# Per-half maxima in an attention softmax: two factors behind the cast and a summed total, in place of a running maximum

## The chip, the cores and the metric

The kernel runs on one core of one Trainium2 chip. The metric is the device time of one execution in microseconds; the time before is the median of three runs. The profile shows one further execution, which also has its own time.

## The reference, cut to what matters

For each of 4 batch rows (2048 positions, width 256, 16 heads of 16), talking-heads attention mixes the heads before and after the softmax. Layer norms and a soft mixture of experts follow; they are untouched by the change.

```python
logits = jnp.einsum('bhid,bhjd->bhij', q, k) * SCALE
logits = jnp.einsum('bhij,gh->bgij', logits, Wpre)
attn = jax.nn.softmax(logits, axis=-1)
attn = jnp.einsum('bhij,gh->bgij', attn, Wpost)
out = jnp.einsum('bhij,bhjd->bhid', attn, v)
```

The softmax runs over 2048 keys. It does not change if a different maximum is subtracted in different parts of the row, as long as each part is rescaled before the sum.

## The kernel before, in words

The work is cut into tiles of 8 query positions x 16 heads = 128 partitions against all 2048 keys. A tile is handled by a `slot`; 16 slots make an iteration, 16 iterations a batch row, and 4 batch rows the kernel: 1024 tiles. The slots are software pipelined: in slot T the engines work on the scores of tile T, on the weights of tile T-1 and on the post-mix of tile T-2. Each engine has its own instruction stream with the order written out by hand in its `slot` function, and semaphores join them. Two halves of the keys are separate: the scores of tile T fill the four banks of `psS`, banks 0 and 1 for the first half, 2 and 3 for the second.

- **TensorE** (L1249 to L1283): scores of columns 0 and 1 (L1179, 12 matmuls, the head mix before the softmax folded into `AH` and `AL`), `turn` of the first half of tile T-2 (L1199, which mixes the heads and puts keys on the partitions, with `rh` and `rl` as weights, into `psP`), scores of columns 2 and 3, and `turn` of the second half. `turn` writes the two banks of `psP` again, so it waits for VectorE's `mixed_low`. Every eighth slot (t = 2 and 10) the product with V (L1214) stands in four pieces between these. The output projection `y` (L1225) is in slot 3 and other row work in slots 11, 12 and 15.
- **ScalarE** (L683): two casts `mixed_high` of `psP` (L653), `bound` (L622, the negative, scaled maximum `nb`), `exps` (L635, the exponentials of a half of the keys and their sum), `highs` (L663, the fp16 cast `ph`); then the same five for the second half, with `factor` (L644, `f0`) between its `exps` and its `highs`.
- **VectorE** (L1021): `half_max` of the first half (L816), the reciprocal of the total of tile T-1 (L848), two `mixed_low` (L830), `low` of tile T-1 (L856, 512 columns), `half_max` of the second half, `row_bound` (L822), two `mixed_low`, and `low` of tile T (L856, 1024 columns). Row work for layer norms stands between (`rows`), and `out_copy` (L840) in slots 3 and 11.
- **GpSimd** (L548): `total` (L517), `mixq` (two L438), `roots`, `first_half` (L524), `post` (L531), `mixq_high` (L446), `post_high` (L540), `mixq_low` (L451), `post_low` (L545), and `low` (L508, the last 512 columns). `roots` are the small steps of two Newton iterations for the layer norms; there are six of them in each of slots 6, 7, 10 and 11, spread over four places (two, one, two, one).

How the softmax is put together before: the first half of the keys is exponentiated against its own maximum, the second against the maximum of both (`row_bound`, a running maximum). One factor `f0 = exp(nb1 - nb0)` carries the first half over, the total is `sums0 * f0 + sums1` in one instruction, and the weights of the halves are `f0 / total` and `1 / total`. The waits that matter:

```python
a.wait_ge(s_mx, T * 3 + 2 * h + 1 + 1)   # bound: second half waits for row_bound
g.wait_ge(s_exp, T * 2 + 2 + 1)          # total
g.wait_ge(s_f, T + 1 + 1)
g.tensor_scalar(tot[:, p:p + 1], sums[:, p, 0:1], f0[:, p:p + 1], sums[:, p, 1:2],
                ALU.mult, ALU.add).then_inc(s_tot, 1)
v.wait_ge(s_tot, T + 1 + 1)              # recip, in VectorE's next slot
```

Of the kernel before, what the change touches and what calls it, by code (L numbers as in the profile page):

```python
# [29 lines left out]
ALU = mybir.AluOpType  # L30
ACT = mybir.ActivationFunctionType
X = mybir.AxisListType.X

P = 128
# [24 lines left out]
LIFT = 14  # L59
# [20 lines left out]
def seq_layer(nc, x, xT, wqk, wv, bqk, bv, wpre, wpost, imask, wout, bout, gamma, beta, mu, scale,  # L80
              w1, b1, w2, b2, cos_t, sin_t, ident_d, out):
    ctx = ExitStack()
    with ctx:
        def sb(name, shape, dt=F32):
            return ctx.enter_context(nc.sbuf_tensor(name, shape, dt))

        def sem(name):
            return ctx.enter_context(nc.semaphore(name))
# [35 lines left out]
        mu_s = sb("mu_s", [P, KT, ES])  # L124
        ident = sb("ident", [P, P])
        ones = sb("ones", [P, P])
        top = sb("top", [P, 2, 3])
        nb = sb("nb", [P, 2, 2])
        sums = sb("sums", [P, 2, 2])
        f0 = sb("f0", [P, 2])  # L130
        tot = sb("tot", [P, 2])
        rr = sb("rr", [P, 2, 2])
        rp = sb("rp", [P, 2, HP])
# [32 lines left out]
        def part(n):  # L166
# [58 lines left out]
        s_A = sem("s_A")  # L225
        s_S = sem("s_S")
        s_mx = sem("s_mx")
        s_exp = sem("s_exp")
        s_nb = sem("s_nb")
        s_f = sem("s_f")  # L230
        s_tot = sem("s_tot")
        s_rec = sem("s_rec")
# [38 lines left out]

        FROM_ONE = [s_A, s_nb, s_f, s_tot, s_rec, s_r0, s_rp, s_rh, s_rl, s_pl, s_plg, s_D, s_F, s_y, s_mx, s_exp, s_ph,
                    s_mh, s_ml, s_oc, s_CTc, s_t1, s_xb, s_st, s_nw, s_out]

        block = ctx.enter_context(nc.Block())
# [9 lines left out]
        def apart(e):  # L287

            e.sem_inc(s_carry, 1)
# [110 lines left out]
        def _(g):  # L400
# [5 lines left out]
            with g.Fori(0, B) as b:  # L406
# [21 lines left out]
                def mixq(it, t, fresh):  # L428

                    T = (b * NIT + it) * TI + t  # L430
                    if not fresh:
                        g.wait_ge(s_S, T * NC - (TG - 1) * NC)
                    g.wait_ge(s_A, T * 4 + 1)
                    for h in range(2):
                        i0 = it * (TI * QI) + (t * QI + h * HQ)
                        v = at[:, :, h * HP:(h + 1) * HP].rearrange("p k (g i) -> p k g i", g=H)
                        apart(g)
                        g.tensor_tensor(v, Q[:, :, bass.ds(i0, HQ)].unsqueeze(2).broadcast_to([P, KT, H, HQ]),  # L438
                                        wpre_q[:, :].unsqueeze(1).unsqueeze(3).broadcast_to([P, KT, H, HQ]),
                                        ALU.mult).then_inc(s_A, 1)  # L440
# [62 lines left out]
                def low(T, t, early):  # L503

                    g.wait_ge(s_ph, T * 2 + 2 + 1)
                    if not early:
                        g.wait_ge(s_D, (T - 1) * 2 + 1)
                    g.tensor_tensor(pl[:, t % 2, NL:N], pr[:, t % 2, NL:N], ph[:, t % 2, NL:N],  # L508
                                    ALU.subtract).then_inc(s_plg, 1)

                def total(T, t):

                    p = t % 2
                    g.wait_ge(s_exp, T * 2 + 2 + 1)
                    g.wait_ge(s_f, T + 1 + 1)
                    apart(g)
                    g.tensor_scalar(tot[:, p:p + 1], sums[:, p, 0:1], f0[:, p:p + 1], sums[:, p, 1:2],  # L517
                                    ALU.mult, ALU.add).then_inc(s_tot, 1)

                def first_half(T, t):  # L520

                    p = t % 2
                    g.wait_ge(s_rec, T + 1 + 1)
                    g.tensor_tensor(rr[:, p, 0:1], rr[:, p, 1:2], f0[:, p:p + 1], ALU.mult).then_inc(s_r0, 1)  # L524

                def post(T, t):

# [20 lines left out]
                def slot(it, t, first, work, live=True):  # L548

                    T = (b * NIT + it) * TI + t  # L550
                    one = not (first and t < 1)
                    t_1 = (t - 1) % TI
                    if one:
                        total(T - 1, t_1)
                    if live:
                        mixq(it, t + LEAD, first and t + LEAD < TG)
                    roots(t, work, 0)
                    if one:
                        first_half(T - 1, t_1)
                        post(T - 1, t_1)  # L560
                    if live:
                        mixq_high(it, t + LEAD)
                    if one:
                        post_high(T - 1, t_1, first and t < 5)
                    if live:
                        mixq_low(it, t + LEAD)
                    if one:
                        post_low(T - 1, t_1)
                    roots(t, work, 1)
                    if one:  # L570
                        low(T - 1, t_1, first and t < 3)
                    roots(t, work, 2)
                    if work is not None and t == POOL_SLOT["bias"]:
                        add_bias(work)
                    roots(t, work, 3)
# [20 lines left out]
        def _(a):  # L596
            barrier(a, 1)
            with a.Fori(0, B) as b:
# [18 lines left out]
                def bound(T, t, h):  # L617

                    p = t % 2
                    m = 2 * h  # L620
                    a.wait_ge(s_mx, T * 3 + 2 * h + 1 + 1)
                    a.activation(nb[:, p, h:h + 1], top[:, p, m:m + 1], ACT.Copy, bias=LIFT * math.log(2.0),  # L622
                                 scale=-SSCALE).then_inc(s_nb, 1)

                def exps(T, t, h, early):
# [13 lines left out]
                def factor(T, t, early):  # L639

                    p = t % 2
                    if not early:
                        a.wait_ge(s_r0, T - 2 + 1 + 1)
                    a.activation(f0[:, p:p + 1], nb[:, p, 0:1], ACT.Exp, bias=nb[:, p, 1:2], scale=-1.0).then_inc(s_f, 1)  # L644

                def mixed_high(T, t, c, Gd):

# [35 lines left out]
                def slot(it, t, first, work, live=True):  # L683


                    T = (b * NIT + it) * TI + t
                    G = (b * NIT + it) * 2
                    early = first and t < 2

                    def mixed(c):  # L690
                        if not (first and t < 2):
                            mixed_high(T - 2, (t - 2) % TI, c, G + (t - 2) // TG)

                    mixed(0)
                    mixed(1)
                    if live:
                        bound(T, t, 0)
                        exps(T, t, 0, early)
                        highs(T, t, 0, early)
                    mixed(2)  # L700
                    mixed(3)
                    if live:
                        bound(T, t, 1)
                        exps(T, t, 1, early)
                        factor(T, t, early)
                        highs(T, t, 1, early)
                    if work is not None and t == ACT_SLOT["turn_u"]:
                        turn(work)
                    if work is not None and t == ACT_SLOT["weigh"]:
                        weigh(work)  # L710
                    if work is not None and t == ACT_SLOT["turn_c"]:
                        store_c(work)
# [26 lines left out]
        def _(v):  # L739
# [39 lines left out]
            with v.Fori(0, B) as b:  # L779
# [36 lines left out]
                    v.tensor_reduce(top[:, t % 2, h:h + 1], psS[:, 2 * h:2 * h + 2, :].rearrange("p c n -> p (c n)"),  # L816
                                    X, ALU.max).then_inc(s_mx, 1)

                def row_bound(T, t):

                    v.wait_ge(s_mx, T * 3 + 2 + 1)
                    v.tensor_tensor(top[:, t % 2, 2:3], top[:, t % 2, 0:1], top[:, t % 2, 1:2], ALU.max).then_inc(s_mx, 1)  # L822

                def mixed_low(T, t, c):

                    v.wait_ge(s_mh, T * NC + c + 1 + 1)
# [17 lines left out]
                def recip(T, t):  # L844

                    p = t % 2
                    v.wait_ge(s_tot, T + 1 + 1)
                    v.reciprocal(rr[:, p, 1:2], tot[:, p:p + 1]).then_inc(s_rec, 1)  # L848

                def low(T, t, h, early):  # L850

# [169 lines left out]
                def slot(it, t, first, work, live=True):  # L1021


                    T = (b * NIT + it) * TI + t
                    two = not (first and t < 2)
                    one = not (first and t < 1) and (live or t < 1)
                    t_1, t_2 = (t - 1) % TI, (t - 2) % TI
                    if live:
                        half_max(T, t, 0)
                    if one:  # L1030
                        recip(T - 1, t_1)
                    rows(t, work, 0)
                    if t % TG == 3 and not (first and t < TG):
                        out_copy((b * NIT + it) * 2 + t // TG - 1, (t // TG + 1) % 2, b * NIT + it - (1 if t < TG else 0))
                    if two:
                        mixed_low(T - 2, t_2, 0)
                        mixed_low(T - 2, t_2, 1)
                    rows(t, work, 1)
                    if one:
                        low(T - 1, t_1, 1, first and t < 3)  # L1040
                    if live:
                        half_max(T, t, 1)
                        row_bound(T, t)
                    rows(t, work, 2)
                    if two:
                        mixed_low(T - 2, t_2, 2)
                        mixed_low(T - 2, t_2, 3)
                    if live:
                        low(T, t, 0, first and t < 2)
                    rows(t, work, 3)  # L1050
# [348 lines left out]
```

## Time and profile before

| what | value |
|---|---|
| median of 3 runs | 8940.56 us (8935.8 to 8940.84) |
| profiled execution, its own time | 8924.24 us |
| its span, first to last instruction | 8922.4 us |
| busy: TensorE, VectorE, ScalarE, GpSimd | 8352.7, 8136.2, 7237.5, 5892.5 us |
| TensorE's mean granted clock | 0.985 of full |

Busy time is what an engine's instructions took, waits at a semaphore left out. An instruction that has started but is held by something on the chip still counts as busy. The time that the kernel takes is decided by which engine others wait for, and that differs between stretches.

### The profile page before, as it was taken

What the parts mean: (1) busy time and instruction counts of PE and PEld (TensorE: products, weight loads), DVE (VectorE), ACT (ScalarE), POOL (GpSimd) and SP (SyncE); (2) the same over time, 40 slices, a digit from 0 to 9 for tenths busy, and PEclk for the clock granted to TensorE, in tenths of its full rate; (3) what the DMA queues carried; (4) which work ended last, traced back from release to release, by engine and by line L of the source; (5) the groups of instructions that cost most, each with busy time, mean ns of one, the idle gap of its engine ahead of it and who ended that gap; (6) DMA issues with size and microseconds to landing.
All of it is one profiled execution on the core that took longest, in us unless ns stands there. A gap on an engine that the chain in (4) does not pass through costs nothing.

```text
span 8922.4 us, 398983 instructions
## 1 busy us (share of the span) xinstructions
PE 8352.7 (94%) x158060; PEld 4650.8 (52%) x158060; DVE 8136.2 (91%) x12237; ACT 7237.5 (81%) x13696; POOL 5892.5 (66%) x12005
## 2 busy tenths in 40 slices
PE   8999999998899999999889999999989999999997
PEld 4555555555455555555545555555554555555554
DVE  7999999997899999999789999999978999999997
ACT  6888888886688888888668888888856888888885
POOL 6666666764666676666466667666646666766673
PEclk9999999999999999999899999999989999999998
DMA  0000000002000000000200000000020000000002
GB/s 31 7 8 8 8 8 8 9 7 73 17 8 8 8 9 7 8 9 8 72 17 8 8 8 9 7 8 9 8 72 17 8 8 8 9 8 8 8 9 76
DMA packets 98673, 141.22 MB, mean 16 GB/s; under 512 B 7840, under 2 KB 88352, under 8 KB 94496
## 3 DMA queue, kind: packets, MB, share of 16 engines
q1 hardware_dynamic: 96800, 115.48, 3.8%
q8 instruction: 1270, 20.81, 1.0%
q14 instruction: 603, 4.94, 0.2%
HBM read 73.51 MB, written 39.85 MB: 13 GB/s over the span
## 4 chain that ended last, share of the span: by engine, by line
DVE 44%; PE 33%; issue 19%; DVEq 2%; ACT 1%; POOL 1%; POOLq 0%; ACTq 0%
PE psS L1179 17%; DVE top L816 14%; DVE big L830 14%; DVE pl L856 9%; PE psP L1199 6%; PE psO L1214 6%; PE psM L1225 1%; DVE top L822 1%; ACT big L653 1%; DVE rr L848 1%; PE psS L1311 1%; PE psS L1340 1%; DVEq L815 0%; DVEq L853 0%; PE psS L1151 0%
## 5 line engine op out<-in xcount | busy, mean ns | idle before, releaser
L830 DVE SCALAR_TENSOR_TENSOR big<-psP,big 128x512 f16<-128x512 f32 x4096 | 2605.9, 675 | 285.0 <-ACT big L653 275.8
L816 DVE TENSOR_REDUCE top<-psS 128x1 f32<-128x1024 f32 x2048 | 2479.7, 1211 | 214.0 <-PE psS L1179 213.7
L653 ACT ACTIVATE big<-psP 128x512 f16<-128x512 f32 x4096 | 2199.2, 589 | 577.5 <-PE psP L1199 572.4
L1179 PE MATMUL psS<-KH,AH 128*128 128x512 f16 x8192 | 2464.3, 383 | 43.5 <-POOL AL L451 41.8
L1179 PE MATMUL psS<-KH,AL 128*128 128x512 f16 x8192 | 2441.9, 380 | 0.0
L1179 PE MATMUL psS<-KL,AH 128*128 128x512 f16 x8192 | 2439.2, 379 | 0.0
L635 ACT ACTIVATE pr<-psS,nb 128x1024 f32<-128x1024 f32 x2048 | 2281.3, 1114 | 69.1 <-ACT nb L622 3.0
L663 ACT ACTIVATE ph<-pr 128x1024 f16<-128x1024 f32 x2048 | 2151.9, 1051 | 32.3
L1199 PEld LDWEIGHTS psP<-rh,ph 64*128 64x128 f16 x32768 | 1434.3, 95 | 1220.1 <-DVE big L830 1036.0
L1199 PE MATMUL psP<-rh,ph 64*128 64x64 f16 x32768 | 1682.5, 192 | 381.8 <-DVE big L830 344.5
L517 POOL TENSOR_SCALAR tot<-sums,f 128x1 f32<-128x1 f32 x1024 | 743.7, 726 | 1946.6 <-ACT f L644 1943.3
L856 DVE TENSOR_TENSOR pl<-pr,ph 128x1024 f16<-128x1024 f32 (+1 forms) x2048 | 2020.2, 986 | 0.0
L1199 PE MATMUL psP<-rh,pl 64*128 64x64 f16 x32768 | 1663.0, 190 | 0.7 <-issue 0.6
L1199 PE MATMUL psP<-rl,ph 64*128 64x64 f16 x32768 | 1662.9, 190 | 0.3 <-issue 0.2
L1199 PEld LDWEIGHTS psP<-rl,ph 64*128 64x128 f16 x32768 | 1463.2, 95 | 1.8 <-issue 1.6
L1199 PEld LDWEIGHTS psP<-rh,pl 64*128 64x128 f16 x32768 | 1462.7, 95 | 1.2 <-issue 1.1
L1179 PEld LDWEIGHTS psS<-KH,AL 128*128 128x128 f16 x8192 | 802.9, 98 | 971.5 <-issue 6.6
L1179 PEld LDWEIGHTS psS<-KL,AH 128*128 128x128 f16 x8192 | 802.8, 98 | 970.1 <-issue 6.6
L508 POOL TENSOR_TENSOR pl<-pr,ph 128x512 f16<-128x512 f32 x1024 | 1210.2, 1182 | 0.0
L1179 PEld LDWEIGHTS psS<-KH,AH 128*128 128x128 f16 x8192 | 629.2, 98 | 608.4 <-POOL AL L451 43.4
L622 ACT ACTIVATE nb<-top 128x1 f32<-128x1 f32 x2048 | 418.2, 204 | 559.1 <-DVE top L822 434.7
L451 POOL TENSOR_TENSOR AL<-at,AH 128x256 f16<-128x256 f32 x1024 | 798.1, 779 | 2.8
(135 smaller groups left out, 7956.0 us busy)
## 6 DMA issues: line engine op xcount, KB each, us to landing
ph<-in_xT SPq DMA_DIRECT2D x16, 512.0 KB, 7.9
xr<-in_x SPq DMA_DIRECT2D x64, 128.0 KB, 2.1
Q<-in_w SPq DMA_DIRECT2D x8, 1024.0 KB, 6.4
out<-V SPq DMA_DIRECT2D x16, 512.0 KB, 3.9
d_x<-x SPq DMA_DIRECT2D x60, 128.0 KB, 1.7
d_xn<-xn SPq DMA_DIRECT2D x60, 128.0 KB, 1.7
d_lg<-lg SPq DMA_DIRECT2D x60, 128.0 KB, 1.7
d_ct<-cT SPq DMA_DIRECT2D x60, 128.0 KB, 1.7
```

What stands on the lines that cost most here:

```text
L451: g.tensor_tensor(AL[:, t % TG, :, :], at[:, :, :], AH[:, t % TG, :, :], ALU.subtract).then_inc(s_A, 1)
L508: g.tensor_tensor(pl[:, t % 2, NL:N], pr[:, t % 2, NL:N], ph[:, t % 2, NL:N], ALU.subtract).then_inc(s_plg, 1)
L517: g.tensor_scalar(tot[:, p:p + 1], sums[:, p, 0:1], f0[:, p:p + 1], sums[:, p, 1:2], ALU.mult, ALU.add).then_inc(s_tot, 1)
L635: a.activation(pr[:, p, h * N2:(h + 1) * N2], psS[:, 2 * h:2 * h + 2, :].rearrange("p c n -> p (c n)"), ACT.Exp, bias=nb[:, p, h:h + 1], s ...
L653: a.activation(PT[:, hf * JH:(hf + 1) * JH, :, 0, i0:i0 + HQ], psP[:, ih, :].rearrange("p (j g i) -> p j g i", j=JH, g=H), ACT.Copy, scale ...
L663: a.activation(ph[:, t % 2, cs], pr[:, t % 2, cs], ACT.Copy).then_inc(s_ph, 1)
L816: v.tensor_reduce(top[:, t % 2, h:h + 1], psS[:, 2 * h:2 * h + 2, :].rearrange("p c n -> p (c n)"), X, ALU.max).then_inc(s_mx, 1)
L830: v.scalar_tensor_tensor(out=PT[:, js, :, 1, i0:i0 + HQ], in0=psP[:, ih, :].rearrange("p (j g i) -> p j g i", j=JH, g=H), scalar=MDROP, in ...
L856: v.tensor_tensor(pl[:, t % 2, cs], pr[:, t % 2, cs], ph[:, t % 2, cs], ALU.subtract)\
L1179: mm = pe.matmul(psS[:, c, :], A_[:, k8, k, :], K_[:, k, c * CW:(c + 1) * CW], start=n == 0, stop=n == 5)
L1199: mm = pe.matmul(psP[:, ih, j * HP:(j + 1) * HP], p_[rows, t % 2, cs], r_[rows, t % 4, hf, :], start=n == 0, stop=n == 2, tile_position=(i ...
L1214: mm = pe.matmul(psO[32 * w:32 * w + 32, q * P:(q + 1) * P], V[:, j, g_, :, :], PT[:, j, g_, :, :], start=j == 0 and q == 0, stop=j == JT - 1,
```

## The change

Each half keeps its own maximum. `row_bound` on VectorE goes, and ScalarE's `bound` of the second half waits for `half_max` alone. GpSimd gets `lower_bound` (the smaller of the two `nb`) at the head of its slot, then `mixq`, and only then `total`, which is now two instructions: both sums times their factors, and their addition. `factor` makes both factors in one instruction, waits for `lower_bound`, and stands behind `highs` of the second half. `weights` makes both weights in one instruction from the reciprocal.

```diff
 # GpSimd
+                def lower_bound(T, t):
+                    p = t % 2
+                    g.wait_ge(s_nb, T * 2 + 2 + 1)
+                    apart(g)
+                    g.tensor_scalar(nm[:, p:p + 1], nb[:, p, 0:1], nb[:, p, 1:2], None, ALU.min).then_inc(s_nm, 1)
+
                 def total(T, t):
                     p = t % 2
                     g.wait_ge(s_exp, T * 2 + 2 + 1)
                     g.wait_ge(s_f, T + 1 + 1)
-                    apart(g)
-                    g.tensor_scalar(tot[:, p:p + 1], sums[:, p, 0:1], f0[:, p:p + 1], sums[:, p, 1:2],
-                                    ALU.mult, ALU.add).then_inc(s_tot, 1)
-
-                def first_half(T, t):
+                    g.tensor_tensor(ws[:, p, :], sums[:, p, :], ff[:, p, :], ALU.mult).then_inc(s_ws, 1)
+                    g.wait_ge(s_ws, T + 1 + 1)
+                    g.tensor_tensor(tot[:, p:p + 1], ws[:, p, 0:1], ws[:, p, 1:2], ALU.add).then_inc(s_tot, 1)
+
+                def weights(T, t):
                     p = t % 2
                     g.wait_ge(s_rec, T + 1 + 1)
-                    g.tensor_tensor(rr[:, p, 0:1], rr[:, p, 1:2], f0[:, p:p + 1], ALU.mult).then_inc(s_r0, 1)
+                    g.tensor_tensor(rr[:, p, :], ff[:, p, :], rc[:, p:p + 1].broadcast_to([P, 2]), ALU.mult)\
+                     .then_inc(s_r0, 1)
...
                     if one:
-                        total(T - 1, t_1)
+                        lower_bound(T - 1, t_1)
                     if live:
                         mixq(it, t + LEAD, first and t + LEAD < TG)
+                    if one:
+                        total(T - 1, t_1)
                     roots(t, work, 0)
                     if one:
-                        first_half(T - 1, t_1)
+                        weights(T - 1, t_1)
                         post(T - 1, t_1)
 # ScalarE
                 def bound(T, t, h):
                     p = t % 2
-                    m = 2 * h
-                    a.wait_ge(s_mx, T * 3 + 2 * h + 1 + 1)
-                    a.activation(nb[:, p, h:h + 1], top[:, p, m:m + 1], ACT.Copy, bias=LIFT * math.log(2.0),
+                    a.wait_ge(s_mx, T * 2 + h + 1 + 1)
+                    a.activation(nb[:, p, h:h + 1], top[:, p, h:h + 1], ACT.Copy, bias=LIFT * math.log(2.0),
                                  scale=-SSCALE).then_inc(s_nb, 1)
...
                 def factor(T, t, early):
                     p = t % 2
+                    a.wait_ge(s_nm, T + 1 + 1)
                     if not early:
                         a.wait_ge(s_r0, T - 2 + 1 + 1)
-                    a.activation(f0[:, p:p + 1], nb[:, p, 0:1], ACT.Exp, bias=nb[:, p, 1:2], scale=-1.0).then_inc(s_f, 1)
+                    a.activation(ff[:, p, :], nb[:, p, :], ACT.Exp, bias=nm[:, p:p + 1], scale=-1.0).then_inc(s_f, 1)
...
                         exps(T, t, 1, early)
+                        highs(T, t, 1, early)
                         factor(T, t, early)
-                        highs(T, t, 1, early)
 # VectorE
-                def row_bound(T, t):
-
-                    v.wait_ge(s_mx, T * 3 + 2 + 1)
-                    v.tensor_tensor(top[:, t % 2, 2:3], top[:, t % 2, 0:1], top[:, t % 2, 1:2], ALU.max).then_inc(s_mx, 1)
...
                     v.wait_ge(s_tot, T + 1 + 1)
-                    v.reciprocal(rr[:, p, 1:2], tot[:, p:p + 1]).then_inc(s_rec, 1)
+                    v.reciprocal(rc[:, p:p + 1], tot[:, p:p + 1]).then_inc(s_rec, 1)
...
                         half_max(T, t, 1)
-                        row_bound(T, t)
```

## Rows read from the trace of the kernel before

**Rows 1.** The page's first part, busy time of each engine.

```profile
PE 8352.7 (94%) x158060; PEld 4650.8 (52%) x158060; DVE 8136.2 (91%) x12237; ACT 7237.5 (81%) x13696; POOL 5892.5 (66%) x12005
```

**Rows 2.** Waits, whole span: who for whom, total us, times, longest us.

```profile
POOL tot L517 <- ACT f L644: 1943.3, 952, 5.2
...
PE psP L1199 <- DVE big L830: 344.5, 520, 2.6
...
POOL rr L524 <- DVE rr L848: 359.7, 724, 1.5
...
POOL rp L531 <- POOL rr L524: 212.7, 1024, 0.5
```

**Rows 3.** Windows: stretch, us, busy us by engine (instructions), clock, DMA.

```profile
4022.20:4152.10 129.90, 124.67 (x2450) 68.79 (x2449) 122.44 (x183) 111.73 (x212) 89.47 (x187) 1.00 0.03 8
4030.30:4068.20 37.90, 35.34 (x602) 18.36 (x597) 37.73 (x63) 34.16 (x65) 28.56 (x61) 1.00 0.03 10
4129.40:4157.40 28.00, 27.98 (x673) 16.83 (x673) 24.08 (x33) 22.11 (x43) 17.06 (x34) 1.00 0.01 4
```

**Rows 4.** The chain that ended last, behind an output product: start, us, what.

```profile
4143.24 1.01 PE psO L1214 x64
4144.24 0.81 PE psP L1199 x48
4145.05 2.70 PE psS L1179 x12
```

**Rows 5.** Groups of instructions by shape: busy us, mean ns, idle time before them.

```profile
L822 DVE TENSOR_TENSOR top<-top 128x1 f32<-128x1 f32 x1024 | 748.0, 730 | 35.5
...
L644 ACT ACTIVATE f<-nb 128x1 f32<-128x1 f32 x1024 | 289.7, 283 | 0.0
```

**Rows 6.** VectorE's timeline in a slot that it paces: start, us, what.

```profile
4045.93 1.21 DVE L816 TENSOR_REDUCE top<-psS 128x1 f32<-128x1024 f32 x1
4047.17 1.04 DVE L822 TENSOR_TENSOR top<-top 128x1 f32<-128x1 f32 x1
4048.14 1.27 DVE L830 SCALAR_TENSOR_TENSOR big<-psP,big 128x512 f16<-128x512 f32 x2
4049.34 1.21 DVE L856 TENSOR_TENSOR pl<-pr,ph 128x1024 f16<-128x1024 f32 x1
```

**Rows 7.** GpSimd's timeline over the same slot and the next one.

```profile
4047.05 1.15 POOL L508 TENSOR_TENSOR pl<-pr,ph 128x512 f16<-128x512 f32 x1
...
4050.07 0.69 POOL L517 TENSOR_SCALAR tot<-sums,f 128x1 f32<-128x1 f32 x1 [1.18 <-ACT f L644]
4050.72 0.76 POOL L438 TENSOR_TENSOR at<-Q,wpre_q 128x128 f32<-128x128 f32 x2
...
4057.60 0.34 POOL L517 TENSOR_SCALAR tot<-sums,f 128x1 f32<-128x1 f32 x1
```

**Rows 8.** ScalarE's timeline from the end of a second turn on.

```profile
4161.00 1.08 ACT L653 ACTIVATE big<-psP 128x512 f16<-128x512 f32 x2
4162.06 0.20 ACT L622 ACTIVATE nb<-top 128x1 f32<-128x1 f32 x1
...
4163.40 0.28 ACT L644 ACTIVATE f<-nb 128x1 f32<-128x1 f32 x1
4163.59 1.05 ACT L663 ACTIVATE ph<-pr 128x1024 f16<-128x1024 f32 x1
4164.54 1.08 ACT L653 ACTIVATE big<-psP 128x512 f16<-128x512 f32 x2
```

**Rows 9.** Single lines: count, duration in ns, min/median/max.

```profile
L822 DVE TENSOR_TENSOR top<-top x1024: 158/879/1146, 86.1 to 8820.4; 128x1 f32<-128x1 f32 x171
...
L517 POOL TENSOR_SCALAR tot<-sums,f x1024: 334/683/1338, 93.7 to 8822.9; 128x1 f32<-128x1 f32 x171
...
L469 POOL TENSOR_TENSOR zq<-yq x192: 185/190/643, 291.0 to 8854.2; 128x1 f32<-128x1 f32 x192
```

**Rows 10.** VectorE's timeline at the start of a batch.

```profile
94.06 0.16 DVE L848 RECIPROCAL rr<-tot 128x1 f32<-128x1 f32 x1 [5.02 <-POOL tot L517]
```

More of the change, by code:

```diff
@@ L126, in seq_layer @@
         ones = sb("ones", [P, P])
-        top = sb("top", [P, 2, 3])
+        top = sb("top", [P, 2, 2])
         nb = sb("nb", [P, 2, 2])
         sums = sb("sums", [P, 2, 2])
-        f0 = sb("f0", [P, 2])
+        nm = sb("nm", [P, 2])
+        ff = sb("ff", [P, 2, 2])
+        ws = sb("ws", [P, 2, 2])
+        rc = sb("rc", [P, 2])
         tot = sb("tot", [P, 2])
@@ L229, in seq_layer @@
         s_nb = sem("s_nb")
+        s_nm = sem("s_nm")
+        s_ws = sem("s_ws")
         s_f = sem("s_f")
@@ L270, in seq_layer @@
         s_out = sem("s_out")
-        FROM_ONE = [s_A, s_nb, s_f, s_tot, s_rec, s_r0, s_rp, s_rh, s_rl, s_pl, s_plg, s_D, s_F, s_y, s_mx, s_exp, s_ph,
+        FROM_ONE = [s_A, s_nb, s_nm, s_ws, s_f, s_tot, s_rec, s_r0, s_rp, s_rh, s_rl, s_pl, s_plg, s_D, s_F, s_y, s_mx, s_exp, s_ph,
                     s_mh, s_ml, s_oc, s_CTc, s_t1, s_xb, s_st, s_nw, s_out]
```

## The prediction

> **What bounds the kernel now.** I start with the share of the engines in the page [rows 1]: TensorE is busy 94% of the span and VectorE 91%, so neither is free to absorb much, and the question is who waits for whom. The waits of TensorE come next [rows 2]: by far the largest is the post-mix transposition (L1199) waiting for VectorE's `mixed_low` (L830), 344.5 us in 520 cases. That is what a faster VectorE can give back, and no more: a TensorE that never waited there would still need its 8352.7 us busy and its other idle time.
>
> The windows show the two regimes [rows 3]. One whole iteration of 16 slots lasts 129.9 us with TensorE busy for 124.7, so 5.2 us are lost (344.5 / 64 iterations = 5.4). In the nearly five slots behind the `y` product, 37.9 us, VectorE is busy 37.7 and TensorE 35.3: VectorE sets the pace. In the 28 us around the first output product TensorE is busy 28.0 and VectorE 24.1. A plain slot on TensorE is two groups of twelve score matmuls at 2.70 us and two turns at 0.81 [rows 4], 7.02 us; the iteration averages 8.1.
>
> Why VectorE is slow is in its timeline [rows 6]. L816 for the second half starts at 4045.93, L822 (the running maximum, one element a partition) at 4047.17, and the next L830 only at 4048.14. L822 alone, 1.04 us, ends at 4048.21; GpSimd's L508 started at 4047.05 and took 1.15 us, so it ended at 4048.20 [rows 7]. The same instruction takes 0.158 us at its shortest [rows 9] and 0.730 in the mean of 1024 [rows 5]; its median is 0.879 [rows 9], so in most slots it waits, and in this one for L508. The Trainium skill's page "SBUF — State Buffer", section "Who interferes with whom", states this: a VectorE instruction with two SBUF inputs and a GpSimd instruction that reads SBUF exclude each other, and the one that starts second waits for the whole of the first. By that rule, the trace agrees here.
>
> **The change, part by part.**
>
> *L822 goes.* On VectorE an instruction moves the next start by its duration less 0.07 (the pair of L830, 1.27 long, by 1.20, rows 6). From L816's start at 4045.93 to L830's at 4048.14 are 2.21 us; less 1.14 for L816 that leaves 1.07 for an L822 of 1.04. So one costs its duration and 0.03: 0.76 us in the mean, 16 x 0.76 = 12.2 us an iteration, on VectorE, and ScalarE's second bound (L622), which waits for it, comes as much earlier. VectorE's need falls from about 122 to 110 us an iteration [rows 3], below TensorE's 124.7. VectorE alone would then cost TensorE nothing: all 344.5 us would come back. The stall could move to the next instruction of its kind, L856, which starts 2.2 us after L822's place (4049.34 against 4047.17, rows 6), while L508 is over after 1.15; taken as 0, at most the 0.57 us that L822 loses now (0.730 - 0.158).
>
> *Lower bound (new) on GpSimd.* One `tensor_scalar` on one element. Its bounds are L517's: 0.34 where nothing holds it, 1.34 where L856 does [rows 9]. GpSimd waits 1.9 us a slot for ScalarE's L644 today (1943.3 us over 1024 slots, rows 2; 1.18 at 4050.07, a slot after root work), so 0.3 is hidden; I take 0.3, by the minimum, since the lower bound falls where VectorE runs L830 and not L856. ScalarE's `factor` now waits for it, and behind it stand the two L653 of the next slot.
>
> *`mixq` moves ahead of the total.* 0.76 us [rows 7] go from behind the total into GpSimd's wait: free there, and the reciprocal is not reached later by it as long as GpSimd gets to it before the factors are there. L446, AL and all behind keep their order.
>
> *The factors move behind the cast L663.* Two elements in place of one, 0.28 us either way [rows 5] (bounds 0.20, the bound's L622, and 0.29). They come one cast later: L663 starts at 4163.59 and the next instruction 0.95 later [rows 8]. The cast itself comes 0.19 earlier. ScalarE's total is unchanged.
>
> *The total is two instructions.* Each `tensor_tensor` of one or two elements lies between 0.19 and 0.64 [rows 9], with a 0.20 us gap where one waits for the other on GpSimd (L531 behind L524, 212.7 us in 1024, rows 2): 0.19 + 0.20 + 0.19 = 0.58 against 0.34 unhindered for L517 (median 0.68, since L856 often holds it). The two-wide weights cost the same 0.19 as L524: 0.
>
> *The ring that the new order makes.* The end of a second turn on TensorE starts ScalarE's casts (L653, 4161.00), bound (4162.06), exponentials, then cast and factors: 4163.40 + 0.95 + 0.28 = 4164.63 [rows 8]. GpSimd starts some 0.2 later (the same gap as above): total done at 4164.85 + 0.58 = 4165.43. Reciprocal (0.16, rows 10) and two `mixed_low` (1.20, rows 6) bring 4166.8. The turn before ended just ahead of 4161.00, and TensorE wants its next second turn 7.02 - 0.81 = 6.2 us later, at 4167.2. So in a plain slot the ring fits, with 0.3 to 0.5 us to spare. Before, factor and total were 1.2 us earlier in it.
>
> *Where it doesn't fit: the Newton steps.* In slots 6, 7, 10 and 11 GpSimd has six small instructions more, about 1.5 us with gaps. There it is full: from L517 at 4050.07 to L517 at 4057.60, 7.53 us without a wait for the factor [rows 7]. New: 7.53 - 0.34 + 0.30 + 0.58 = 8.07, 1.05 over TensorE's slot. The first of a run starts with GpSimd's idle time in hand (1.9 less the new 0.3 and a little, 1.5), so it ends up some 0.5 late, which the ring's spare swallows; the second (slot 7) is 1.0 late for real. Slot 10 lies under the output product, which adds four times 1.01 us on TensorE [rows 4], and slot 11 is again a first one. That leaves 1.0 us an iteration. I add 0.5 for small VectorE work between reciprocal and L830 (`variances` in slot 5, the output copy in 3 and 11), which the short spare no longer hides: 1.5 x 60 = 90 us.
>
> *Starts and ends of the four batches.* At a start VectorE waits 5.02 us for the total [rows 10], which now has the lower bound and `mixq` in front of it; at an end the last factors are a cast later. About 1.5 + 1.0 us, 4 times: 10 us.
>
> *Sum.* -344.5 + 90 + 10 = -244.5 us. The profiled execution took 8924.24: 8679.7. The median of the runs is 8940.56, 16.3 above it; I carry that over: **8696 us**, 2.7% less.
>
> **Rivals.**
>
> *A. TensorE alone sets the time.* The late totals of slot 7 vanish because slot 8 and the lead of TensorE's scores absorb them. For it: TensorE already runs without a gap around an output product (27.98 of 28.00) [rows 3] although VectorE needs 8 us a slot elsewhere, so there is more elasticity than my spare. 8940.6 - 344.5 + 10 = 8606. This is the low end.
>
> *B. GpSimd becomes the bound in every slot.* If L856 (1.21 us, rows 6) gets in between L508 and the lower bound or `mixq`, GpSimd waits it out each slot. The full slot of 7.53 us less 1.5 of root work is 6.0, the holds of L856 in it counted; new instructions add 0.54, the wait for the reciprocal 0.35 (359.7 us over 1024, rows 2), a lower bound held in full up to 0.6 more: 6.9 to 7.5, and 8.1 to 8.7 with root work. With 0.2 us a slot over TensorE in ten slots and 1.3 in three that is 5.9 us an iteration, less 1 to 4 of slack: a gain of 0 to 230 us, about 110: 8830. For it: L517 has a median of 0.683 against 0.34 unhindered, so GpSimd meets L856 there today. Against: with L822 gone L508 starts before L856 by a wide margin, and in TensorE's pace two L830 lie between. The page named above gives the rule by which this would happen: its lock is exclusive and held for a whole instruction, so new GpSimd instructions can lose 1.1 us each; by it alone the sum would be this 8830.
>
> *C. Slower.* One mechanism: the lower bound falls behind L856 (1.34 us instead of 0.3), ScalarE stands at `factor`, and L653, which TensorE needs, stands behind it. It decides once the factor is later than today's slot of 8.1 us allows: the ring of 6.7 us (with the turn itself) would need 1.4 us more in nearly every slot, not just the 1.0 that one L856 costs. With two of them, 0.1 us over 8.1 in 900 slots: 9030.
>
> *D. The gain is under 0.2%*: B at its worst; 8925 to 8940.
>
> **How the numbers follow.** 0.2% (18 us) is about what a measurement of this kernel can tell from no change. My own case 0.45 (8650 to 8780), A 0.20 (8600 to 8650), B 0.20 (8780 to 8920), D 0.08, C 0.07. The likeliest is my own: 8696. The range for 8 in 10 goes from A's end, 8600, to 8890, inside B. Faster 0.84, same 0.09, slower 0.07.
>
> **What would show it.** In the profile after: L822's row gone and VectorE's busy time about 750 us lower; TensorE's wait for L830 down from 344.5 to about 100 us; L856's mean unchanged within 0.1; GpSimd's largest wait still that for the factor (shorter, some 1 us a slot), and a new wait of VectorE's reciprocal for the total that is concentrated in slots 7, 8 and 12. B would show as GpSimd busy or held without waits for the factor, and the reciprocal waiting in most slots; C as a wait of L644 for the lower bound in most slots; A as TensorE's wait near nothing. I am wrong on mechanism if TensorE still waits 250 us or more.

## The result and the profile after

The median went from 8940.19 to 8837.6 us, a ratio of 0.9891 (95% interval 0.9878 to 0.9905): 1.1% faster, where 2.7% were forecast. The direction was right and the size was less than half. The profiled execution took 8836.91 us, its span 8835.1.

The page's first part, as [rows 1], and the waits of the whole span, as [rows 2]:

```profile
PE 8342.3 (94%) x158060; PEld 4654.2 (53%) x158060; DVE 7730.8 (88%) x11213; ACT 7314.1 (83%) x13696; POOL 6557.3 (74%) x14053
```

```profile
POOL nm L521 <- ACT nb L636: 494.7, 396, 4.8
POOL ws L528 <- ACT ff L659: 474.5, 619, 2.2
...
PE psP L1208 <- DVE big L840: 274.1, 432, 3.0
...
DVE rc L858 <- POOL tot L530: 164.8, 195, 6.3
...
ACT ff L659 <- POOL nm L521: 99.8, 128, 5.5
```

TensorE still waits 274.1 us for `mixed_low` (now L840) where I forecast about 100; the prediction had named 250 or more as the sign of a wrong mechanism. VectorE's busy time fell by 405 us, not by the 748 that L822 had. GpSimd is busy 665 us longer. ScalarE's `factor` (L659) waits for the lower bound 128 times, about twice an iteration, and VectorE's reciprocal for the total 195 times. As forecast, that wait is concentrated in slots 7, 8 and 12: 45.9, 66.5 and 19.5 of the 164.8 us.

The groups of instructions show where 227 of VectorE's missing 343 us went (count, busy us, mean ns), and what `mixq` takes now:

```profile
L866 DVE TENSOR_TENSOR pl<-pr,ph 128x1024 f16<-128x1024 f32 x1024 | 1306.2, 1276 | 0.0
L443 POOL TENSOR_TENSOR at<-Q,wpre_q 128x128 f32<-128x128 f32 x2048 | 1241.2, 626 | 9.2 <-POOL AL L456 5.0 <-issue 2.3 <-POOL Q L429 1.6
...
L866 DVE TENSOR_TENSOR pl<-pr,ph 128x512 f16<-128x512 f32 x1024 | 850.0, 830 | 0.0
...
L973 DVE TENSOR_TENSOR colmax<-colmax,lg 128x256 f32<-128x256 f32 x64 | 70.7, 1104 | 0.0
...
L909 DVE TENSOR_SCALAR ir<-vr 128x2 int32<-128x2 int32 x64 | 57.2, 894 | 0.1
```

In the kernel before, the same instructions were (the groups of that trace; L856 is now L866, L438 is L443, L963 is L973, L899 is L909):

```profile
L856 DVE TENSOR_TENSOR pl<-pr,ph 128x1024 f16<-128x1024 f32 x1024 | 1238.1, 1209 | 0.0
...
L856 DVE TENSOR_TENSOR pl<-pr,ph 128x512 f16<-128x512 f32 x1024 | 782.2, 764 | 0.0
L438 POOL TENSOR_TENSOR at<-Q,wpre_q 128x128 f32<-128x128 f32 x2048 | 781.9, 400 | 7.0 <-POOL AL L451 5.0 <-POOL Q L424 1.5
...
L963 DVE TENSOR_TENSOR colmax<-colmax,lg 128x256 f32<-128x256 f32 x64 | 26.3, 411 | 0.0
...
L899 DVE TENSOR_SCALAR ir<-vr 128x2 int32<-128x2 int32 x64 | 10.0, 156 | 0.1
```

The hold moved. VectorE's L909 went from 156 to 894 ns and L973 from 411 to 1104, both forms of L866 took 0.07 us more, and on GpSimd `mixq` (L443) went from 400 to 626 ns. In the trace before, no L899 and no L963 starts more than 0.1 us ahead of the end of GpSimd's L508: L822 stood in front of them and took the hold. In the trace after, 56 of the 64 L909 and 60 of the 64 L973 start inside GpSimd's L513, and end 0.02 to 0.03 and 0.28 to 0.29 us behind its end. VectorE's timeline in slot 13, and GpSimd's beside it, show the first kind:

```profile
4058.70 1.21 DVE L831 TENSOR_REDUCE top<-psS 128x1 f32<-128x1024 f32 x1
4059.84 1.25 DVE L973 TENSOR_TENSOR colmax<-colmax,lg 128x256 f32<-128x256 f32 x1
4061.01 1.27 DVE L840 SCALAR_TENSOR_TENSOR big<-psP,big 128x512 f16<-128x512 f32 x2
```

```profile
4059.65 1.15 POOL L513 TENSOR_TENSOR pl<-pr,ph 128x512 f16<-128x512 f32 x1
4060.79 0.45 POOL L521 TENSOR_SCALAR nm<-nb 128x1 f32<-128x1 f32 x1
```

L973 stands where L822 stood, right behind the maximum of the second half. It starts at 4059.84 inside GpSimd's L513 (to 4060.80), and ends 0.29 us behind that, at 4061.09.

**Where TensorE waits, slot by slot.** The idle time of TensorE ahead of its turns (L1199, after L1208), summed over the trace by the slot that the scores before it belong to. The first turn and the second are apart, the figures are mean us per iteration of the 60 with row work, and figures under 0.05 are left out. The two last columns are totals in us: the four first iterations of the batches, which have no row work, and the turns behind the last scores of a batch. The first turn of a slot waits for the `mixed_low` pair at the end of VectorE's slot before, so a late row instruction of slot 5, 8 or 13 shows in slot 6, 9 or 14. The second turn waits for the pair right behind the reciprocal, so a late total shows there.

```
slot            0    1    3    6    7    8    9    14   15   sum   | first its.  ends
before  turn 1  .29  .53  -    .43  .93  -    .75  .86  .81  4.60  |
        turn 2  -    -    -    -    -    -    .30  -    -    0.31  |  38.8      34.2
after   turn 1  -    -    -    .31  -    -    .83  .70  -    1.84  |
        turn 2  -    -    .32  -    .71  .78  .30  -    -    2.18  |   1.6      35.0
```

Before: 4.91 x 60 + 38.8 + 34.2 = 368 us. After: 4.02 x 60 + 1.6 + 35.0 = 278 us. The difference is 90 us, and the spans differ by 87, but they aren't made of the same waits. Of the 38.8 us in the first iterations 22.0 are waits for GpSimd's `rl` (4 times, at the starts of the batches). After the change TensorE waits 21.8 us for ScalarE's `pr` at its scores, where it was 1.4, so most of these 22 only moved. The wait for `mixed_low` fell by 70.4 us (16.8 to 1.6 of it in the first iterations), and TensorE's busy time by 10.4. The windows confirm the iterations without row work. The first iteration of the second batch and the one behind it, in the kernel before and in the kernel after:

```profile
2299.95:2427.56 127.61, 117.44 (x1984) 60.87 (x1985) 109.66 (x147) 102.51 (x193) 89.16 (x176) 0.97 0.01 2
2427.56:2557.86 130.30, 124.94 (x2455) 68.95 (x2450) 122.44 (x183) 111.73 (x212) 89.99 (x187) 1.00 0.02 6
```

```profile
2276.91:2399.62 122.71, 116.71 (x1985) 60.57 (x1985) 101.58 (x132) 103.23 (x193) 102.60 (x206) 0.97 0.01 3
2399.62:2528.71 129.09, 124.81 (x2454) 68.96 (x2449) 116.23 (x167) 112.89 (x212) 100.26 (x219) 1.00 0.02 6
```

In this pair of windows the iteration without row work gains 4.9 us, the one with it 1.2.

### The profile page after: what moved, and what is told of

Its sections match the earlier page's. It is cut to its first block, busy times and chain, and to the rows that moved or that the text cites. A ratio compares the mean times of both kernels' runs of the same rounds, so it can differ in the third digit from the quotient of the medians.

```text
span 8835.1 us, 399633 instructions
## 1 busy us (share of the span) xinstructions
PE 8342.3 (94%) x158060; PEld 4654.2 (53%) x158060; DVE 7730.8 (88%) x11213; ACT 7314.1 (83%) x13696; POOL 6557.3 (74%) x14053
## 4 chain that ended last, share of the span: by engine, by line
PE 51%; DVE 21%; issue 16%; POOL 7%; ACT 4%; DVEq 1%; POOLq 1%; ACTq 0%
PE psS L1188 29%; PE psP L1208 11%; DVE big L840 6%; PE psO L1223 6%; DVE pl L866 5%; DVE top L831 5%; ACT big L668 3%; PE psM L1234 1%; POOL rh L553 1%; POOL zr L476 1%; POOL zr L474 1%; PE psS L1320 1%; PE psS L1349 1%; POOL at L443 1%; POOL rl L558 1%
## 5 line engine op out<-in xcount | busy, mean ns | idle before, releaser
L840 DVE SCALAR_TENSOR_TENSOR big<-psP,big 128x512 f16<-128x512 f32 x4096 | 2614.6, 678 | 439.7 <-ACT big L668 424.8
L866 DVE TENSOR_TENSOR pl<-pr,ph 128x1024 f16<-128x1024 f32 (+1 forms) x2048 | 2156.2, 1053 | 0.0
L1208 PEld LDWEIGHTS psP<-rh,ph 64*128 64x128 f16 x32768 | 1433.0, 95 | 1102.1 <-DVE big L840 852.3
L1208 PE MATMUL psP<-rh,ph 64*128 64x64 f16 x32768 | 1681.2, 192 | 284.0 <-DVE big L840 274.1
L1208 PE MATMUL psP<-rh,pl 64*128 64x64 f16 x32768 | 1661.3, 190 | 2.6 <-issue 2.5
L1208 PE MATMUL psP<-rl,ph 64*128 64x64 f16 x32768 | 1661.2, 190 | 0.4 <-issue 0.2
L1208 PEld LDWEIGHTS psP<-rh,pl 64*128 64x128 f16 x32768 | 1461.3, 95 | 3.7 <-issue 3.5
L1208 PEld LDWEIGHTS psP<-rl,ph 64*128 64x128 f16 x32768 | 1461.9, 95 | 2.1 <-issue 2.0
L443 POOL TENSOR_TENSOR at<-Q,wpre_q 128x128 f32<-128x128 f32 x2048 | 1241.2, 626 | 9.2 <-POOL AL L456 5.0
L513 POOL TENSOR_TENSOR pl<-pr,ph 128x512 f16<-128x512 f32 x1024 | 1196.1, 1168 | 0.0
L521 POOL TENSOR_SCALAR nm<-nb 128x1 f32<-128x1 f32 x1024 | 413.1, 403 | 501.4 <-ACT nb L636 494.7
```

The costliest lines, as they stand in the source:

```text
L840: v.scalar_tensor_tensor(out=PT[:, js, :, 1, i0:i0 + HQ], in0=psP[:, ih, :].rearrange("p (j g i) -> p j g i", j=JH, g=H), scalar=MDROP, in ...
L866: v.tensor_tensor(pl[:, t % 2, cs], pr[:, t % 2, cs], ph[:, t % 2, cs], ALU.subtract)\
L1208: mm = pe.matmul(psP[:, ih, j * HP:(j + 1) * HP], p_[rows, t % 2, cs], r_[rows, t % 4, hf, :], start=n == 0, stop=n == 2, tile_position=(i ...
```

## The experiments

Three theories stood against each other at first. Theory 1: GpSimd is late in the slots with Newton steps, the lower bound with it, and ScalarE's `factor` and casts stand behind. Theory 2: L822's stall sits on VectorE's row work now. Theory 3: the ring of factor and total has become too long in plain slots too. The table above already speaks against theory 3, since slots 0, 1, 4, 5 and 10 to 13 lose nothing in the kernel after.

Times are medians; the ratios are to the kernel before, which each group of runs took again on its own chip (8930 to 8937 us). "After" stands at 0.9891 (0.9878 to 0.9905), beside a kernel before at 8940.19. A difference to it in us can therefore be off by about 10 us, and where the intervals of the ratios overlap the two versions are not told apart.

**One: the lower bound ahead of the last Newton steps.** In slot 7 of the kernel after, GpSimd's and ScalarE's timelines read:

```profile
4009.61 1.16 POOL L513 TENSOR_TENSOR pl<-pr,ph 128x512 f16<-128x512 f32 x1
4010.73 1.17 POOL L476 TENSOR_TENSOR zr<-zr,vr 128x2 f32<-128x2 f32 x1
4012.10 0.19 POOL L479 TENSOR_SCALAR zr<-zr 128x2 f32<-128x2 f32 x1 [0.20 <-POOL zr L476]
4012.38 0.19 POOL L481 TENSOR_TENSOR yr<-yr,zr 128x2 f32<-128x2 f32 x1
4012.59 0.28 POOL L521 TENSOR_SCALAR nm<-nb 128x1 f32<-128x1 f32 x1
4012.87 0.76 POOL L443 TENSOR_TENSOR at<-Q,wpre_q 128x128 f32<-128x128 f32 x2
4013.59 0.20 POOL L528 TENSOR_TENSOR ws<-sums,ff 128x2 f32<-128x2 f32 x1
```

```profile
4011.06 1.06 ACT L678 ACTIVATE ph<-pr 128x1024 f16<-128x1024 f32 x1
4012.91 0.29 ACT L659 ACTIVATE ff<-nb,nm 128x2 f32<-128x2 f32 x1 [0.79 <-POOL nm L521]
4013.11 1.06 ACT L668 ACTIVATE big<-psP 128x512 f16<-128x512 f32 x2
```

A Newton step of 0.19 us lasts 1.17 behind VectorE's L866, the lower bound is late by that, and `factor` stands 0.79 us with the casts for TensorE behind it. So the edit moves the lower bound ahead of those steps.

```diff
-                        lower_bound(T - 1, t_1)      # head of slot T
...
                         low(T - 1, t_1, first and t < 3)
+                    if not drain:
+                        lower_bound(T, t)            # end of slot T
                     roots(t, work, 2)
```

> The kernel after, with GpSimd's lower bound of tile T moved to the end of slot T, ahead of the last three Newton steps (they follow it), in place of the head of slot T+1. Theory 1 (GpSimd is late in root slots: ScalarE's factor stands for the lower bound, 99.8 us in 128 cases, and the casts L668 stand behind the factor): that wait goes to under 20 us, TensorE's wait for L840 falls from 274 to about 170, time 8837 - 100 = 8740. Theory 2 (the stall of the removed L822 sits now on VectorE's row instructions L909, L933 and L973): nothing of that is touched, 8825 to 8840. Theory 3 (the longer ring of factor and total is too long in plain slots as well): unchanged, 8830 to 8840.

Measured 8869.64, ratio 0.9927 (0.9914 to 0.9941): 32 us slower than after. The wait of `factor` went as expected, but nothing was gained:

```profile
DVE rc L858 <- POOL tot L530: 212.9, 259, 6.3
ACT nb L636 <- DVE top L831: 146.3, 254, 9.8
ACT ff L659 <- POOL nm L521: 25.4, 12, 5.6
```

The Newton steps now stand between the lower bound and the total, so VectorE's reciprocal waits longer (212.9 us against 164.8). TensorE's wait in slots 7 and 8 is 0.88 + 0.84 us, and 0.44 is new in slot 11. Theory 1 in this form falls: this order within GpSimd doesn't help. What is left of it is the amount of work ahead of the total, which run four tries.

**Two: VectorE's row work away from L822's old place.**

```diff
-                    rows(t, work, 2)
                     if two:
                         mixed_low(T - 2, t_2, 2)
                         mixed_low(T - 2, t_2, 3)
+                    rows(t, work, 2)
```

> The kernel after, with VectorE's row work of place 2 (L909, L933, L973, L983 and bn_stats) moved behind the two mixed_low of the second half, away from GpSimd's L513. Theory 2: L909 falls from 0.89 to 0.16 us in the mean and L973 from 1.10 to 0.41; of the 1.7 us an iteration that reach the path about 1 comes back at TensorE, 60 iterations: 8837 - 60 = 8775. Theory 1: the mean of L909 and L973 falls but slots 6 to 9 stay late: 8820 to 8837. Theory 3: 8830 to 8840.

Measured 8803.23, ratio 0.985 (0.9835 to 0.9865): 34 us faster than after. L973 is back at 426 ns and L909 at 396. Slots 6 and 14 lose 0.08 and 0.04 us in place of 0.31 and 0.70, while slot 15 gets 0.34; the sum is 3.44 in place of 4.02, and 0.58 x 60 = 35 us. The moved hold is real and worth this much, a little over half of the 60 us that I had expected. Slot 9 keeps 1.09 of its 1.13 us.

**Three: both moves.**

> Both moves together: the lower bound ahead of the last Newton steps, and VectorE's row work behind the second pair of mixed_low. If theories 1 and 2 are both right and separate places: the sum of the two gains, about 8680. If only one is right: the time of that one run alone. Theory 3: no more than 20 us from 8837.

Measured 8841.89, ratio 0.9897 (0.9882 to 0.9912), no different from after. The two effects add with their signs: +32 - 34.

**Four: two Newton iterations in place of three** (`NEWTON = 2`, with the steps spread as 1, 1, 1, 1 over the four places). The kernel makes three Newton iterations for each of its two roots, where its description above speaks of two in all. The roots of this version are less exact, so it is a probe and no replacement.

> The kernel after with two Newton iterations for each root in place of three (the inverse roots of the layer norms are less exact: that part of the computation is cut by a third; the rest is as in the reference). Each root slot has four small GpSimd instructions in place of six. Theory 1: 2 x 0.25 us less in each of slots 6, 7 and 11 gives back 0.5 to 1.5 us an iteration: 8837 - 60 = 8775, and the factor's wait for the lower bound falls to a third. Theory 2: L973 in slot 13 unchanged, L909 may change as GpSimd's phase does: 8800 to 8837. Theory 3: 8830.

Measured 8775.35, ratio 0.9819 (0.9806 to 0.9833): 62 us faster than after. Slots 7 and 8 lose 0.30 + 0.27 us in place of 0.71 + 0.78, and slots 6, 9 and 14 are unchanged (0.34, 0.84 + 0.30, 0.71). Two small instructions less in a slot give back 0.9 us an iteration: GpSimd's amount of work in the root slots is on the path.

**Five to eight: the order, part by part.** The change has two halves: other maxima (with lower bound, two factors and a total of two steps) and another order (`factor` behind the cast, `mixq` ahead of the total). Each half was undone alone or in part.

```diff
 # five, ScalarE
+                        factor(T, t, early)
                         highs(T, t, 1, early)
-                        factor(T, t, early)
```

```diff
 # six, GpSimd
                         lower_bound(T - 1, t_1)
+                        total(T - 1, t_1)
                     if live:
                         mixq(it, t + LEAD, first and t + LEAD < TG)
-                    if one:
-                        total(T - 1, t_1)
```

Seven has both of these edits, and eight has the new order in the kernel before, with the running maximum and `f0` kept.

> The kernel after with one part undone: ScalarE's factor stands ahead of the cast of the second half, as before the change. Theory 3 (the ring is 0.95 us too long with the factor behind the cast): the total is ready 0.95 us earlier, VectorE's reciprocal waits less (164.8 us now) and the time falls by 50 to 100: 8760. Theory 1: the factor needs the lower bound 0.95 us sooner and so stands longer for it, in plain slots too; the wait of L659 for L521 rises from 100 us to 300 or more and the time rises: 8870 to 8930.

Measured 8866.68, ratio 0.9929 (0.9916 to 0.9943), 29 us slower than after. The reciprocal waits less (104.7 us), as theory 3 had it, but the wait of `factor` for the lower bound is 336.0 us in 278 cases. The cast in front of it is useful cover.

> The kernel after with one part undone: GpSimd makes the total ahead of mixq. Theory 1: mixq (0.76 us) falls behind the wait for the factor, GpSimd's work per slot grows by what it used of that wait, root slots are 0.7 us later each and the time rises: 8870 to 8920. Theory 3: in root slots GpSimd reaches the total 0.76 us sooner, the reciprocal's wait shrinks, 8800. Theory 2: within 20 us of 8837.

Measured 8809.38, ratio 0.9867 (0.9852 to 0.9883), 28 us faster than after by the medians and 21 by the ratios, whose intervals just touch; TensorE's waits ahead of its turns are 36 us less in its trace. That is against theory 1's expectation. Theory 3 had about this time, but by a shorter wait of the reciprocal, and that wait is longer (200.5 us). Slots 7 and 8 are worse, as theory 1 says (0.97 + 1.14 us). But with GpSimd in another phase `mixq` isn't held (405 ns against 626), nor are L909 and L973 (154 and 462 ns), and slots 6, 9 and 14 lose 0.00, 0.64 and 0.06 us in place of 0.31, 1.13 and 0.70.

> Only the maximum is changed: separate maxima, lower bound, two factors and the two-step total, but the factor ahead of the cast and the total ahead of mixq, as in the kernel before. It says what the removal of L822 is worth without the new order. Theory 1: lower bound, factor and total now stand in one chain on the path of both engines; the gain over before (8940) is small or gone: 8900 to 8980. Theory 3: the short ring is kept and L822 is gone: 8750.

Measured 8914.68, ratio 0.9984 (0.9975 to 0.9993). `factor` waits 377.7 us for the lower bound; slots 7 and 8 lose 1.22 + 1.20.

> The kernel before with the new order alone: the factor behind the cast and mixq ahead of the total; running maximum and one-step total stay. VectorE sets the pace there, so by all theories nothing is gained on VectorE; if the ring had no spare at 8.1 us a slot it would be slower. Theory 1 and 2: 8930 to 8960. Theory 3: 8990 or more, since the ring is 0.95 us longer in every slot.

Measured 9004.03, ratio 1.0083 (1.0069 to 1.0097): slower, in the size that theory 3 had, though not in plain slots. The reciprocal waits 74.8 us in place of 27.8, and slots 3, 8 and 9 lose more (0.35, 0.16 and 1.45 us in place of 0, 0 and 1.05). So the new order costs 0.8% with the running maximum and gives 0.9% (0.9891 / 0.9984) without it. By itself neither half pays more than 0.2%. Of the new order it is `factor` behind the cast that pays (run six keeps it, run five undoes it), not `mixq` ahead of the total.

**Nine: the hold itself.** If L822 is dear because it has two inputs in SBUF, one input should do.

```diff
-                    v.tensor_tensor(top[:, t % 2, 2:3], top[:, t % 2, 0:1], top[:, t % 2, 1:2], ALU.max).then_inc(s_mx, 1)
+                    v.tensor_reduce(top[:, t % 2, 2:3], top[:, t % 2, 0:2], X, ALU.max).then_inc(s_mx, 1)
```

> The kernel before with one line changed: the running maximum is a tensor_reduce over the two half maxima (one SBUF input) in place of a tensor_tensor with two. Theory P (L822's cost is the hold by GpSimd's L508, and an instruction with one SBUF input isn't held): L822 falls from 0.73 us in the mean to about 0.15, VectorE needs 9 us an iteration less, the short ring and the one-step total stay, and the row instructions then meet the hold as in the kernel after; TensorE's wait for L830 falls from 344 to about 200: 8790. Rival P' (any small VectorE instruction there waits, or the 1.04 us are its own): L822 stays at 0.7 and the time at 8940.

Measured 8816.44, ratio 0.9872 (0.9857 to 0.9887). Its line in this trace, count and min/median/max ns:

```profile
L822 DVE TENSOR_REDUCE top<-top x1024: 154/155/159, 86.3 to 8711.6; 128x1 f32<-128x2 f32 x171
```

No L822 out of 1024 waits any more, where the median was 879 ns. It isn't that GpSimd is out of the way: 675 of them start over 0.3 us ahead of the end of L508, and take 154 to 159 ns. In the kernel before 683 do, and each of these ends 0.01 to 0.02 us behind L508's end, after 1131 ns in the median. So the wait was the hold by L508, and the `tensor_reduce` with one input doesn't have it. One changed line of the kernel before does as much as the whole change. The hold moves here too: L963 takes 902 ns, L899 678, L923 1167 (472 before) and L973 999 (342 before), and slot 9 loses 1.87 us in place of 1.05.

**Ten to twelve: relief for GpSimd where the Newton steps are.**

```diff
 # GpSimd
-                        low(T - 1, t_1, first and t < 3)
+                        if work is None or t not in (6, 7, 11):
+                            low(T - 1, t_1, first and t < 3)
 # VectorE, behind its own low of tile T-1
+                        if live and work is not None and t in (6, 7, 11):
+                            v.tensor_tensor(pl[:, t_1 % 2, NL:N], pr[:, t_1 % 2, NL:N], ph[:, t_1 % 2, NL:N],
+                                            ALU.subtract).then_inc(s_plg, 1)
```

> The kernel after, but in the three slots with Newton steps that no output product covers (6, 7, 11) VectorE also makes the last 512 columns of low, and GpSimd's L513 (1.15 us) is left out there. Theory 1b (GpSimd's whole work in root slots makes the total late, whichever instruction comes first): TensorE's waits in slots 7 and 8, now 0.71 + 0.78 us, fall below 0.3 together, 60 iterations: 8837 - 70 = 8767. Rival (VectorE's row work is what is late in slots 7 to 9): VectorE has 0.67 us more in each, and the time rises to 8870 or more.

Measured 8851.2, ratio 0.991 (0.9894 to 0.9925), 14 us above after and not told apart from it. GpSimd is no longer late (the reciprocal waits 35.6 us, `factor` 26.4), but VectorE is: its added instruction takes 946 ns, held as well, and TensorE's loss in slots 7 and 8 moves to the first turns (0.91 + 0.04, with 0.19 left of the second), with 0.44 new in slot 12.

> The relief of slots 6, 7 and 11 on top of the kernel with the total ahead of mixq (8809). Theory 1b: its waits of TensorE in slots 7, 8 and 13 (0.97, 1.14, 0.23 us) all but go: 8809 - 120 = 8690. Rival (VectorE's row work): 8809 to 8850.

Measured 8721.23, ratio 0.9764 (0.9751 to 0.9777), the fastest version. With the total ahead of `mixq` the same relief pays 88 us, most of it in slots 7 and 8 (2.11 to 0.86 us an iteration). L910 and L974, the row instructions at L822's old place, aren't held (154 and 422 ns), but in run six they weren't either, and the added instruction takes 842 ns against 946 in run ten. Why the relief pays here and not there isn't shown. The waits:

```profile
PE psP L1212 <- DVE big L841: 161.2, 436, 3.0
...
ACT ff L660 <- POOL nm L522: 59.1, 68, 5.6
DVE rc L859 <- POOL tot L531: 54.0, 147, 6.1
```

> The relief on top of the one-input running maximum. With the short ring GpSimd is late only little in root slots: theory 1b says a gain of no more than 40 us over that kernel; the rival (VectorE's row work) says it loses about 30 us.

Measured 8887.74, ratio 0.9951 (0.9938 to 0.9965), 71 us slower than the one-input maximum alone. With the short ring GpSimd wasn't late, and the relief only loads VectorE: slots 7, 8 and 12 lose 1.12, 0.27 and 0.45 us where they lost 0.00, 0.03 and 0.00.

## Why the prediction was wrong

Outcome: 1.1% where 2.7% were forecast, 142 us too low. Two steps were wrong in size: that all of TensorE's wait would come back, and that the hold of L822 would move nowhere. By the prediction's steps:

- **"All 344.5 us would come back."** Mis-sized from the start, by 52 us. 34 us of the turns' waits lie behind the last scores of the four batches, and every version has them (34 to 36); another 18 us, 0.30 x 60 of the second turn in slot 9, are the least that any version has there. A total over the span is no measure of what a loop can give.
- **L822 goes, 12.2 us an iteration on VectorE.** Right for the instruction. In the iterations without row work nearly all of the wait for `mixed_low` came back: 16.8 us to 1.6. That part of the sum held, and so did the ring in a plain slot, where TensorE loses nothing.
- **"The stall could move to L856; taken as 0."** This is the step that failed. I looked 2.2 us ahead to L856 and passed over what stands at L822's very place in slots 4, 5, 8, 9, 13 and 14, VectorE's row work of place 2. L909 and L973 are held as L822 was, by 0.74 and 0.69 us in the mean, and L933 in slot 8 by 0.22 (694 ns for 472). Slots 6, 9 and 14, just behind, lost 2.34 us before and 2.14 after, 128 us in all. Moving that row work (run two) gave 34 us; 18 of the rest are those of every version, and the other 76, mostly in slot 9, aren't put down to one cause.
- **The lower bound, 0.3 us.** Right in plain slots (median 279 ns); 403 ns in the mean.
- **`mixq` moves for free.** Wrong on GpSimd: it moved under L866 and takes 626 ns in place of 400, twice a slot, 459 us of GpSimd in all. 473 of the 2048 are held (12 before), mainly in slots 0, 1, 3, 4, 10, 11 and 13, where TensorE loses nothing but in slot 3. The price on the path is another: undoing the move alone (run six) took 1.44 us an iteration from slots 6, 9 and 14, added 0.89 in slots 7, 8, 12 and 13, and gained 21 to 28 us.
- **The Newton steps, 1.0 us an iteration.** Right in place, short in size: slots 7 and 8 lose 0.71 + 0.78 us. I had let the first root slot end within the spare. Steps of 0.19 us held for 1.1 behind L866 use it up. Slots 11 and 12, which I named too, lose nothing. Slot 3, where the output copy stands between reciprocal and `mixed_low`, loses 0.32, within the 0.5 that I had added.
- **Starts and ends, 10 us.** At the ends about 1 us (34.2 to 35.0). At the starts the reciprocal's longest wait grew from 5.3 to 6.3 us, and TensorE's wait for `rl` became one for `pr`, 22.0 us against 20.4 more.

Added up: predicted to remain were 90 us in the loop; measured are 241 there and 35 at the ends. The 241 are 128 in slots 6, 9 and 14, 89 in slots 7 and 8 (60 forecast), 19 in slot 3 (30 forecast for it and its like), and 4 elsewhere.

**The rivals.** B's number, 8830, was near, but not its mechanism: GpSimd was to set every slot, with the reciprocal waiting in most. The reciprocal waits in 195 of 1024, and plain slots run at TensorE's pace. What B said of holds is right for part of the instructions: `mixq`, the lower bound (173 of 1024) and the Newton steps are held, but `mixq` mainly in slots where TensorE loses nothing. A holds only for the iterations without row work. C's mechanism (`factor` behind a late lower bound) exists, 99.8 us in 128 cases, but removing it (run one) made nothing faster. The Trainium skill's rule in "SBUF — State Buffer", section "Who interferes with whom", was the right tool: run nine agrees with it on 1024 instructions. It should have been applied to each VectorE instruction that could come to stand beside L508, not to the next large one.

**Open:** how the remaining loss of slots 7 to 9 divides between the holds and plain work on the two engines. In run four less GpSimd work there gained, in run ten more VectorE work cost what the relief of GpSimd gave; no run took the holds away alone.

## What to carry to other kernels

When an instruction is dear because another engine holds it, removing it passes the hold on to whatever takes its place in the order: list those instructions slot by slot, small and rare ones too. Before that, try the same operation in a form with one SBUF input; here one line did as much as a change of four engines' order. And read a wait as a table by place in the loop before promising it back: ends of batches and slots with extra work don't belong to the plain slot's account.

## What the hardware showed that was not expected

- A VectorE `tensor_scalar` on two integers a partition (L909, one SBUF input) is held by GpSimd too: 894 ns in the mean, 156 in the kernel before. So not only two-input instructions are; the `tensor_reduce` with one input never was, in 1024 cases. The same section of the Trainium skill's page names `tensor_scalar` among those that can take the shared pair, and this trace agrees. The same operation on one integer a partition isn't held: in run nine 56 of the 64 L943 start over 0.3 us ahead of the end of L508, and take 153 to 156 ns.
- A hold works on tiny GpSimd instructions as on large ones: the Newton steps L474 and L476 took 1087 and 1188 ns at most against some 195 in the median. The total's addition L530 never took more than 257 ns, but none of the 1024 starts while L866 runs: L528 stands right ahead of it, and it is L528 that starts inside L866 (110 times).
- A wait on one engine can be a phase lock between two others: with the total ahead of `mixq` GpSimd waits 1156.6 us for the factors in place of 474.5, and the kernel is no slower. GpSimd then meets neither L866 with `mixq` (12 of 2048 held) nor L909's and L973's counterparts with L513 (154 and 462 ns).
